# Adaptive-norm block with two attentions and a spline feed-forward: the first loads taken alone, eight sorting slots instead of four, chunk loads on ScalarE's queue, and four score banks in the first batch

## What is computed

```python
# conv: causal, depthwise, 8 taps (cond), bias;  x: (8, 256, 512)
x = x + attn1(conv(x), qkv_w, qkv_b, out_w, out_b, alibi)   # 16 heads of 32, causal, softmax
x = x + ffn(attn2(x, mask=cond, Wq, Wk, Wv))                # 16 heads of 16 over the 512 columns

def spline(cp, out, inp):          # cubic through control points -> dense weight
    n = out * inp; t = linspace(0, len(cp) - 1, n); i = floor(t); f = t - i
    p0, p1, p2, p3 = cp[i - 1], cp[i], cp[i + 1], cp[i + 2]
    return (0.5 * (2*p1 + (p2-p0)*f + (2*p0-5*p1+4*p2-p3)*f**2
                   + (3*p1-p0-3*p2+p3)*f**3)).reshape(out, inp)

def ffn(h):                        # gate, up: (2048, 512); down: (512, 2048), all by spline
    return (silu(h @ gate.T) * (h @ up.T)) @ down.T
```

## Time and profile before

| | us |
|---|---|
| median of three runs | 1350.14 |
| lowest and highest of them | 1348.1, 1355.51 |
| the profiled execution | 1351.68 |
| its span, first to last instruction | 1349.9 |

### The profile page before, as it was taken

The page is one execution under the profiler, slowest core; times in us unless marked ns, Lnnn a source line. Parts: engine busy times, 40 slices in busy tenths (PEclk is TensorE's granted clock), DMA queues, the critical chain, the costliest instruction groups (busy, mean ns, idle before and its releaser), DMA issues.

```text
span 1349.9 us, 21318 instructions
## 1 busy us (share of the span) xinstructions
PE 1222.1 (91%) x7656; PEld 681.7 (50%) x7656; DVE 777.9 (58%) x1173; ACT 520.9 (39%) x698; POOL 353.7 (26%) x203
## 2 busy tenths in 40 slices
PE   2686679999999999999999999999999999999988
PEld 2353225655455545556355555556356555555436
DVE  5675553558644684457734684458725586356822
ACT  0332046323543255332643245332643236342562
POOL 3075293047000920038000830028000650000000
PEclk9889569999999999999999999999899999999999
DMA  6788723267043732267043642258042650348024
GB/s 252 227 289 330 179 72 75 61 165 219 18 110 131 175 120 58 56 172 230 23 110 122 161 142 48 66 162 241 22 110 96 139 191 15 97 148 231 18 110 172
DMA packets 81063, 180.99 MB, mean 134 GB/s; under 512 B 14468, under 2 KB 54356, under 8 KB 71284
## 3 DMA queue, kind: packets, MB, share of 16 engines
q1 hardware_dynamic: 76144, 166.81, 42.6%
q10 hardware_dynamic: 3552, 8.67, 1.7%
q0 software_dynamic: 1280, 4.20, 0.8%
...
## 4 chain that ended last, share of the span: by engine, by line
PE 71%; DVE 8%; SPq 7%; DMA 5%; issue 3%; ACT 3%; POOL 3%; DVEq 0%; ACTq 0%; POOLq 0%
PE psum L1151 9%; PE psum L1103 9%; PE psum L929 7%; PE psum L969 6%; SPq L413 5%; PE psum L970 4%; PE psum L971 4%; PE psum L958 4%; PE psum L1063 4%; PE psum L947 3%; PE psum L935 3%; DVE max L837 3%; PE psum L1138 3%; PE psum L1027 3%; PE psum L1043 2%
## 5 line engine op out<-in xcount | busy, mean ns | idle before, releaser
L837 DVE TENSOR_REDUCE max<-psum 128x1 f32<-128x512 f32 x512 | 327.7, 684 | 119.9 <-PE psum L1103 116.7
L675 ACT ACTIVATE probs<-psum 128x1024 f32<-128x1024 f32 x256 | 247.9, 1022 | 174.5 <-PE psum L1138 173.2
L1103 PE MATMUL psum<-k,q 52*128 52x512 f32 x512 | 187.1, 507 | 34.1 <-DMA k<-low 20.6
L546 POOL TENSOR_TENSOR h<-h_in,tap 128x1024 f32<-128x1024 f32 x7 | 13.3, 1897 | 606.4 <-DVE low L741 606.4
L1103 PEld LDWEIGHTS psum<-k,q 52*128 52x128 f32 x512 | 78.2, 194 | 167.9 <-DVE max L837 126.0
L1151 PE MATMUL psum<-probs,v 128*32 128x512 f32 x1024 | 140.3, 621 | 0.4 <-ACT probs L675 0.3
L1138 PE MATMUL psum<-q,k 54*128 54x512 f32 x512 | 114.1, 443 | 15.6 <-DMA q<-max_l 8.1
L556 POOL TENSOR_TENSOR h<-h,products 128x1024 f32<-128x1024 f32 x49 | 121.8, 2485 | 3.8
L969 PE MATMUL psum<-stack 128*128 128x512 f32 x256 | 113.7, 444 | 0.0
L739 DVE CAST high<-low 128x1024 fp32r<-128x1024 f32 x32 | 22.9, 716 | 143.5 <-ACT low L575 116.3
L929 PE MATMUL psum<-h,qkv_w 128*128 128x256 f32 x448 | 103.5, 384 | 0.0
...
## 6 DMA issues: line engine op xcount, KB each, us to landing
stack<-wd_sorted SPq DMA_DIRECT2D x64, 1024.0 KB, 6.6
stack<-high SPq DMA_DIRECT2D x128, 128.0 KB, 2.4
...
q<-high SPq DMA_DIRECT2D x128, 64.0 KB, 4.2
k<-high SPq DMA_DIRECT2D x128, 64.0 KB, 2.5
...
wd_sorted<-q SPq DMA_DIRECT2D x4, 1024.0 KB, 8.8
```

The costliest lines, as they stand in the source:

```text
L675: nc.scalar.activation(probs[:, u // 2 % 2, u % 2 * 2:u % 2 * 2 + 2, :], psum[:, 2 + u % 2 * 2:4 + u % 2 * 2, :], ACT.Exp)\
L837: nc.vector.reduce_max(max2[:, g, e, i, t:t + 1], psum[:, SCORE_BANKS[s], :], AX_X).then_inc(S["s2_max"], 1)
L1103: nc.tensor.matmul(psum[:, SCORE_BANKS[s], :], r(q2[rows, g, i, t * P:(t + 1) * P]), r(k2[rows, g, i, :]), start=True, stop=True).then_inc ...
```

## The change

1. ACT waits for the first sequence, the taps and the conv bias before it issues its seven loads; SP waits for the last quarter of ACT's weights before it issues the segment mask and what stands behind it.
2. Each of the eight sorted tiles has a slot of its own: tiles 0 to 3 (`EARLY`) in `q2` and `k2` as before, tiles 4 to 7 in `stack1`. POOL's gathers of tiles 4 to 7 wait for PE's last use of `q1` and `k1` instead of for the stores. On ACT the rounding of tiles 4 to 7 moves behind the copy of the second attention's queries, on DVE the subtraction moves behind the split of its keys, and on SP their stores move behind the copies for head group 1. SP waits for the stores of tiles 0 to 3 only before it writes to `q2` and `k2`, and for tiles 4 to 7 before it writes to `stack1` again.
3. Chunk 0 waits for `natural_stored` instead of `second_out`. Chunks 3 to 7 are loaded by ACT: 3 and 4 behind the first attention's exponentials, 5 to 7 behind the copies of the second attention's values.
4. In batch 0 `max_rows(b, 0)` is issued behind head group 2 instead of behind group 3, the loads of the next batch's residual and mask.
5. In batch 0 the first 28 scores rotate over banks 0, 1, 3 and 4. `shifted(0)` and `shifted(1)`, which write banks 2 to 5, then also wait for 28 maxima.

```diff
@@ -55,3 +55,4 @@
 RING = 3
-SORT = 4
+SORT = NT
+EARLY = 4
 
@@ -82,3 +83,12 @@
                                if x in SCORE_BANKS else -1))
-LAST_IN_BANK = [max((r for r in range(s) if SCORE_BANKS[r] == SCORE_BANKS[s]), default=None) for s in range(NS)]
+
+
+FIRST_BANKS = [(0, 1, 3, 4)[s % 4] if s < WINDOW_SCORES - 4 else SCORE_BANKS[s] for s in range(NS)]
+
+
+def last_in_bank(banks):
+    return [max((r for r in range(s) if banks[r] == banks[s]), default=None) for s in range(NS)]
+
+
+LAST_IN_BANK, FIRST_LAST_IN_BANK = last_in_bank(SCORE_BANKS), last_in_bank(FIRST_BANKS)
 QK1_FROM = 1 + (NS - WINDOW_SCORES) // 4
@@ -239,3 +249,4 @@
         sort_slots = [t[:].rearrange("p g i n -> p (g i n)")[:, 2048 * i:2048 * (i + 1)]
-                      .rearrange("p (a g n) -> p a g n", a=2, g=2) for t in (q2, k2) for i in range(2)]
+                      .rearrange("p (a g n) -> p a g n", a=2, g=2) for t in (q2, k2) for i in range(2)] \
+            + [stack1[:, i] for i in range(NT - EARLY)]
 
@@ -322,5 +333,3 @@
                 u, q = c // 4, c % 4
-                if c == 0:
-                    sp.wait_ge(second_out, NQ)
-                elif c == 1:
+                if c < 2:
                     sp.wait_ge(natural_stored, 16 * NQ)
@@ -343,2 +352,3 @@
                 sp.dma_start(dst, src).then_inc(small_loaded, 16)
+            sp.wait_ge(qk_loaded[CT - 1], 16)
             for i in range(2):
@@ -369,7 +379,3 @@
                 load_chunk(c)
-            for n in range(SORT):
-                store_sorted(n)
-            for c in range(3, 5):
-                load_chunk(c)
-            for n in range(SORT, NT):
+            for n in range(EARLY):
                 store_sorted(n)
@@ -393,4 +399,4 @@
                 if first:
-                    for k in range(SORT):
-                        sp.wait_ge(sorted_stored[k], 16 * len(range(k, NT, SORT)))
+                    for k in range(EARLY):
+                        sp.wait_ge(sorted_stored[k], 16)
                     for e in range(2):
@@ -423,4 +429,7 @@
                     stacks2(g)
-                    if first and g < 3:
-                        load_chunk(5 + g)
+                    if first and g == 1:
+                        for n in range(EARLY, NT):
+                            store_sorted(n)
+                    if first and g == 2:
+                        max_rows(b, 0)
                     if not first:
@@ -435,3 +444,2 @@
                     load_mask(cond[b])
-                max_rows(b, 0)
                 if first:
@@ -439,3 +447,6 @@
                     sp.dma_start(zt[:], z_table).then_inc(zt_loaded, 16)
+                    for k in range(EARLY, NT):
+                        sp.wait_ge(sorted_stored[k], 16)
                 else:
+                    max_rows(b, 0)
                     sp.wait_ge(S["sum_ready"], fed(b, "sum_ready", LT))
@@ -511,4 +522,2 @@
             def gather(n):
-                if n >= SORT:
-                    pool.wait_ge(sorted_stored[n % SORT], 16 * (n // SORT))
                 for g in range(2):
@@ -531,3 +540,4 @@
                 gate_up_chunk(c)
-            for n in range(SORT, NT):
+            pool.wait_ge(S["t1_ready"], H1 // 2)
+            for n in range(EARLY, NT):
                 gather(n)
@@ -564,2 +574,4 @@
         def _(act):
+            act.wait_ge(S["x_loaded"], 16)
+            act.wait_ge(conv_loaded, 32)
             for c in range(CT):
@@ -625,5 +637,12 @@
 
+                def load_chunk(c):
+                    u, q = c // 4, c % 4
+                    act.wait_ge(gate_up_step, 3 * (c - 1))
+                    cols = slice(q * 256, (q + 1) * 256)
+                    act.dma_start(gu_chunks[c % 2][0], gu_basis[:, :, cols]).then_inc(chunk_loaded[c % 2], 16)
+                    act.dma_start(gu_chunks[c % 2][1], gu_points[:, u, :, cols]).then_inc(chunk_loaded[c % 2], 16)
+
                 if first:
                     act.wait_ge(natural_stored, 16 * NQ)
-                    for n in range(SORT):
+                    for n in range(EARLY):
                         sort_high(n)
@@ -638,4 +657,4 @@
                 if first:
-                    for n in range(SORT, NT):
-                        sort_high(n)
+                    for c in range(3, 5):
+                        load_chunk(c)
 
@@ -651,2 +670,4 @@
                 if first:
+                    for n in range(EARLY, NT):
+                        sort_high(n)
                     act.wait_ge(ones_made, 2)
@@ -664,3 +685,6 @@
 
-                if not first:
+                if first:
+                    for c in range(5, N_GEN):
+                        load_chunk(c)
+                else:
                     feed(b)
@@ -801,3 +825,3 @@
 
-                for n in range(SORT if first else 0):
+                for n in range(EARLY if first else 0):
                     sort(n)
@@ -817,4 +841,2 @@
                 for t in range(LT):
-                    for n in range(SORT + 2 * t, SORT + 2 * t + 2) if first else ():
-                        sort(n)
                     wait("proj_ready", t + 1)
@@ -832,2 +854,4 @@
                 split(b, 1, "high2", "low2")
+                for n in range(EARLY, NT if first else EARLY):
+                    sort(n)
 
@@ -836,3 +860,4 @@
                     g, e, i, t = s // GS, s % 2, s % GS // (2 * CT), s // 2 % CT
-                    nc.vector.reduce_max(max2[:, g, e, i, t:t + 1], psum[:, SCORE_BANKS[s], :], AX_X).then_inc(S["s2_max"], 1)
+                    bank = (FIRST_BANKS if first else SCORE_BANKS)[s]
+                    nc.vector.reduce_max(max2[:, g, e, i, t:t + 1], psum[:, bank, :], AX_X).then_inc(S["s2_max"], 1)
 
@@ -1087,2 +1112,4 @@
                 def scores(s):
+                    banks = FIRST_BANKS if first else SCORE_BANKS
+                    last_in_bank = (FIRST_LAST_IN_BANK if first else LAST_IN_BANK)[s]
                     g, n = s // GS, s % GS
@@ -1092,9 +1119,9 @@
                             wait("aug_rows", 64)
-                    if s < 2:
+                    if s < len(set(banks[:WINDOW_SCORES])):
                         wait("v2_out", CT)
-                    elif LAST_IN_BANK[s] is None:
+                    elif last_in_bank is None:
                         wait("max2_low", 2)
                     else:
-                        wait("s2_max", LAST_IN_BANK[s] + 1)
-                    if SCORE_BANKS[s] == 7 and s >= WINDOW_SCORES + 4 * (OUT_AT[0] - 1):
+                        wait("s2_max", last_in_bank + 1)
+                    if banks[s] == 7 and s >= WINDOW_SCORES + 4 * (OUT_AT[0] - 1):
                         wait("y_out", 1)
@@ -1102,3 +1129,3 @@
                     rows = slice(e * ROWS2, e * ROWS2 + MAX2)
-                    nc.tensor.matmul(psum[:, SCORE_BANKS[s], :], r(q2[rows, g, i, t * P:(t + 1) * P]),
+                    nc.tensor.matmul(psum[:, banks[s], :], r(q2[rows, g, i, t * P:(t + 1) * P]),
                                      r(k2[rows, g, i, :]), start=True, stop=True).then_inc(S["s2_ready"], 1)
@@ -1130,3 +1157,5 @@
                         wait("max2_low", 1)
-                        if not first:
+                        if first:
+                            wait("s2_max", WINDOW_SCORES - 4)
+                        else:
                             pe.wait_ge(S["inter_out"], fed(b, "inter_out", NT))
```

## The result

The changed kernel takes **1338.76 us** (median of 4 runs, 1329.74 to 1344.19), the kernel before, run beside it, 1350.58 (4 runs, 1348.1 to 1355.51). The ratio on record is 0.9881, with a 95% interval of 0.9844 to 0.9918; it is not the quotient of the two medians, which is 0.9912. The direction was right, the size was not: 1308 was forecast with a range of 1300 to 1320, and the gain is 12 us by the medians and 16 by the ratio, instead of 42. The profiled execution took 1340.07.

A forecast was written before the change was run, and what follows sets the result against it. PE's batches of 154.2 us bound the kernel, unchanged, so only the first 209.8 us counted. Gains 19.4 + 24.5 - 1.7 = 42.2 off 1351.68 gave 1309.5; 1.5 for the median made it 1308, range 1300 to 1320.

The forecast's parts named there:

- Part 1: Start, through ACT's query and key copies: with loads held back they end at 26.8 instead of 46.2 us, gain 19.4.
- ACT ends 1.4 later: At the start, ACT's query and key copies were taken to end 1.4 us after PE's instructions behind the last lane tile.
- The second way of adding it up: ACT's own chain at the start: 22.2 + 1.3 for its table + 3.03 puts its end at 26.5 us.
- Part 2: Down weight: quarters shift as a whole, chunk 0 no longer competes with the last natural store; off the path, counted 0.
- Part 3: Sorted tiles: SP no longer waits for the last store, first scores at 129.5 instead of 144.8 us (old clock).
- 1.8 to the scores: From the end of group 0's copies on SP to the first scores: 1.8 us, from the old trace.
- The four subtractions: On DVE before the first maximum: 1.23 to 2.3 us each, ending between 128.3 and 132 us (old clock).
- Part 4: Scores and rows of maxima: `shifted(0)` at 152 instead of 176.5 us (old clock), gain 24.5, bounds 26 and 18.
- just hidden: 4 MB of stores ahead of group 2 in SP's queue: 10.6 us from 135.4, so 146, costing the rows nothing.
- Part 5: Next batch's convolution: starts at 152, L929 at 187 us (old clock), 1.7 given back, bounds 0 and 6.
- (a): Rival: the next convolution becomes the bound, chunks taking 14 or 16 us to land; 1316 or 1320 us, chance 0.15.

The follow-up runs named there:

- the start alone: Kernel before with only ACT's two waits and SP's wait at the start added: 1342.16 us, ratio 0.9907.
- the first run with both the rows and the stores moved: Changed kernel, group 1's rows of maxima ahead of SP's loads, stores of sorted tiles 4 to 7 on ACT behind chunk 7: 1322.61 us, 0.9764.
- the run with small chunks: Changed kernel loading only 32 of 256 columns of chunks 3 to 7, all instructions and waits kept: 1337.62 us, 0.9877.
- the third execution of the changed kernel: Changed kernel unedited, a third look of one execution: 1325.97 us, L954 reached at 182.4.
- the rest alone: Changed kernel without the three waits at the start (ACT's two and SP's): 1349.34 us, ratio 0.9944.

## Why the prediction was wrong

**What held.** What bounds the kernel, and where the change acts, was read rightly: all of the gain lies ahead of the first L954; behind it the instructions are the same, and the time differs by the dips of the granted clock. The start of the convolution (5.3, measured 5.41), its length, and ACT's wait without a cost of its own held. Steps with an order on SP (5.3 us for the fixed rows, measured 113.92 - 108.66 = 5.3; 9.2 for group 0's copies, measured 9.6) held too.

**Part 1, its end.** PE ended its last quarter at 25.1, forecast 25.0. The step that failed is "ACT ends 1.4 later": 1.4 us is the time from PE's end to the *start* of ACT's copies (41.78 to 43.17 in the earlier trace rows), and their own 3.03 us were left out. The second way of adding it up starts ACT's table load at 22.2, while PE was still at work; it started at 25.19. Measured: 26.48 to 29.50. An adding error, 2.7 us.

Of the next 2.8 us, 1.9 are what POOL takes from DVE. I had counted POOL's coefficients against the convolution and nothing against what follows. Now POOL's additions to the residual and mask run beside DVE's splits, where in the kernel before they had been over for 12 us. DVE's timeline behind ACT's copies:

```profile
28.08 0.69 DVE L763 CAST high<-low 128x1024 fp32r<-128x1024 f32 x1 [0.62 <-ACT low L587]
28.81 1.23 DVE L765 TENSOR_TENSOR low<-low,high 128x1024 f32<-128x1024 f32 x1
29.95 2.84 DVE L763 CAST high<-low 128x1024 fp32r<-128x1024 f32 x1
32.83 1.94 DVE L765 TENSOR_TENSOR low<-low,high 128x1024 f32<-128x1024 f32 x1
```

The second pair is the same work as the first and takes 2.86 us more, beside this instruction of POOL and its successors:

```profile
29.13 3.11 POOL L501 TENSOR_TENSOR x<-x,out_bias 128x1024 f32<-128x1024 f32 x1 [1.95 <-DMA x<-in_x_rows]
```

That is the port pair that the prediction cited from the Trainium skill (SBUF — State Buffer, Who interferes with whom), and the rows agree: a cast of 0.69 us took 2.84. I used the rule for the instructions that the change separates and not for those that it brings together. DVE's first row of the natural tiles starts 5.2 us behind ACT's copies, 3.3 in the kernel before. The other 0.9 us are PE's: DVE came late to free the buffer, PE stood idle for 3.18 us, and its granted clock was 0.50 (1.2 GHz) from 37.1 to 39.4 us. The changed kernel first, then the same 16 instructions in the kernel before, at a granted clock of 1.00 (2.4 GHz):

```profile
37.17 3.64 PE L1271 MATMUL psum<-v,inv 32*128 32x512 f32 x16 [3.18 <-DVE probs L933]
```

```profile
51.97 2.00 PE L1242 MATMUL psum<-v,inv 32*128 32x512 f32 x16 [1.29 <-DVE probs L908]
```

Gain 16.7 instead of 19.4 at ACT's copies, 13.9 at the last natural tile, the edge of the bounds (14 to 20).

**Part 2, counted at 0.** Chunks 0 and 1 are now loaded together with the gathers, at 59.85, and the first exponential, which stands behind the rounding of four gathered tiles on ACT, came 2.3 us later than the shift says. That the chunks beside the gathers did it is likely and not shown: from DVE's last natural tile to this exponential it takes 27.3 us in the kernel before, 28.3 with the start alone (its chunk 0 as before), 29.5 in the changed kernel, and 27.5 in the first run with both the rows and the stores moved, which has the chunks in the same place.

**Part 3, the landing.** "1.8 to the scores" is the term that was mis-sized: it was taken from a row in which SP's queue was alone, after the kernel had waited for all its stores and before chunk 5 was asked for. The change lets ACT ask for chunks 5 and 6 at 117.75, in the middle of these copies. It measured 6.9 us (123.52 to 130.44), and from first copy to first maximum 17.3 instead of 11.7; the run with small chunks gives it back (12.2). From its own issue to its landing such a copy took 2.3 us before (133.9 to 144.9 us) and 7.3 in the changed kernel (117.5 to 130.3), by the medians of these rows:

```profile
k<-low SPq DMA_DIRECT2D x2, 64.0 KB, 2.3
```

```profile
k<-low SPq DMA_DIRECT2D x3, 64.0 KB, 7.3
```

The four subtractions, which the sum had as the last to end before the first maximum, ended at 121.5 and held up nothing. The 5.4 us at the reciprocals belong to no step: a wait that the kernel before shows with 2.26 us comes with 5.9 to 9.6 in sum in a third of the executions.

**Part 4, SP's way to the rows.** I let the group 2 copies take 7.5 us behind four stores, and took them as "just hidden". In the profiled execution of the changed kernel this held: the copies took 7.8 us, and SP and DVE were even (rows issued at 142.68, maxima turned at 142.01), because the maxima were late too. It did not hold in general. In 9 of the 15 profiles that have the stores at this place SP came to the rows 3 to 10 us after the maxima were turned, as in the third execution of the changed kernel (copies 13.8 us) and with small chunks (12.4). There, less traffic or sooner reciprocals ran into the list.

**Part 5.** L954 waited for nobody, so 1.7 us did not have to be given back; but the stretch behind `shifted(0)` took 38.3 instead of 33.3 us, because the rows of group 1 stood in SP's queue behind a table of 1 MB and needed 8.86 us. The run with these rows sooner has the wait of 4.77 us gone. In the kernel before the same table stands ahead of the same rows on SP's list, but it was issued at 175.36 and the rows at 182.44, 7 us later; now it is issued at 157.21 and the rows at 158.43. I had moved the maxima and the rows closer and not asked what stood between them on the list. The convolution, which part 5 was about, began at 149.1 where the prediction had 132.6, 14.8 of it inherited, and ended at 183.8: still ahead of L954.

**The rivals.** (a) gave 1316 to 1320, and its mechanism, not its number, is what the runs with the rows sooner show once the other waits are gone; in the changed kernel itself it does not show. None of the rivals had the copies late ahead of the first scores, or a wait for the second rows; the range ended at 1320 because only the convolution was let be late. And 7.8 us of the miss in the profiled execution (22.0 at L954 and 7.8 behind it are the 29.8 by which its span missed) are the batches behind, which I had taken as fixed from one execution and which differ by 6 us between three executions of the changed kernel alone.

**The two halves.** By their ratios the start alone brings 0.9% and the rest alone 0.6%, where the prediction had 19.4 us (1.4%) and 22.8 us (1.7%). So most of the miss lies in parts 3 to 5. Three waits stand in a row (the start's weights, the last sorted store, the rows), and the sum of 42.2 took each as gone whole: with the start alone, 16.7 us gained at ACT's copies are 12.4 at SP's fixed rows and 10.8 at the next batch.
